# A quarter of the score masks goes from VectorE to ScalarE and GpSimd, with all order lists remade

## The chip, the cores and the metric

The kernel runs on one core of a Trainium2 chip. The metric is the device time of one execution in microseconds (us). Five engines matter: TensorE (PE, with its weight loads as PEld), VectorE (DVE), ScalarE (ACT), GpSimd (POOL) and SyncE (SP), which only issues DMAs here.

## The reference, cut to what matters

Sixteen sequences (batches) of 512 tokens by 256 features go through a block: layer norm, causal linear attention with 16 heads of 16, residual, layer norm, a mixture of experts with one shared and eight routed experts, residual.

```
q, k = elu(x Wq^T) + 1, elu(x Wk^T) + 1 ;  v = x Wv^T
out_i = q_i . sum_{j<=i} k_j v_j^T / (q_i . sum_{j<=i} k_j + 1e-8)
x = x + out Wo^T
x = x + sum_e cw[n,e] * (silu(x Wg_e) * (x Wu_e)) Wd_e + shared expert
```

## The kernel before

Each batch is cut into 4 chunks of 128 tokens. Within a chunk, attention is computed as a 128x128 matrix of scores per head, which is masked causally, and multiplied with v; across chunks it goes through running sums of k v^T ("state", used by "inter"). Products in reduced fp32 are made three times, of high and low halves (x3 in "scores", "k", "q", "gate", "up", "down").

The work is a list of named entries `name.i.b` for each engine (i: which part, b: which batch). Each engine runs its own list in order and waits on semaphores. `FIRST` is the start, `STEP` is repeated for t = 3 to 15 with the last number as a lag (batch t minus lag), and `LAST` is the end. The lists and the table `BANK`, which says which of six PSUM banks each product uses, are data; the code of the entries does not change.

The entries that the change and the prediction speak of:

- `piece.n` splits a loaded part of the weights: ScalarE copies the high half, GpSimd (for n=0 VectorE) subtracts it for the low half. Pieces 0 and 1 hold the weights of q and k, 2 and 3 those of v and of the output, 4 to 8 those of gate and up (pieces of 128x1024, the last 128x512), 9 to 11 those of down.
- `k.i`, `q.i`: TensorE's projection; ScalarE makes relu and exp (L661, L664); VectorE adds them (L861). `k_split.i`: ScalarE copies k_hi (L680), GpSimd subtracts for k_lo (L755). `q_split.i`: ScalarE q_hi (L674, two), VectorE q_lo (L867, two). `cum.i` is a scan on VectorE (L908).
- `scores.i` (i = 0 to 3, L1163) fills four banks at a time, and waits for k_lo, q_lo and for the four banks to be drained.
- `mask.j` (j = 0 to 15) drains the bank of one 128x512 tile of scores into the SBUF ring `scores` of 8 tiles. On VectorE it is one instruction that multiplies by the causal mask (L916). If `mask.j` stands in ScalarE's and GpSimd's lists, ScalarE copies the tile (L693), which frees the bank, and GpSimd then multiplies in SBUF (L767). `values.i` (L1180) waits for its four masked tiles.
- `gate`, `up`, `weigh` (L776), `split` (L725, L779) and `down` are the experts. A bank of `up.i` is drained by VectorE (L1018).
- `state`, `inter`, `wo`, `router`, `turn`, `warm`: the state products, their use, the output projection, the router, TensorE transposes, and idle transposes that only keep TensorE busy in the start.

In the kernel before, batches 0 and 1 send the odd masks (1, 3, ..., 15) through ScalarE and GpSimd; batches 2 to 15 have all 16 on VectorE.

Of the kernel before, what the change touches and what calls it, by code (L numbers as in the profile page):

```python
# [55 lines left out]
        q_split.0.0 up.1.2 q.1.0 result.0.3 mask.0.0 mask.3.0 den.0.0 mask.1.0 mask.2.0 at.1.1 den.1.0
        gate.4.2 at.0.1 gate.3.2 state.0.0 gate.5.2 up.4.2 up.5.2 wo.1.1 up.3.2 wo.0.1 ln2_stats.0.1
        mask.4.0 mask.7.0 ln2_apply.0.1 blocks.1.1 mask.5.0 mask.6.0 ln1_stats.0.-1 q_split.1.0 gate.8.2
        gate.7.2
# [8 lines left out]
        turn.1.0 turn.0.0 warm.8.0 k.0.0 q.0.0 k.1.0 v.0.0 v.1.0 q.1.0 scores.0.0 k_turn.0.0 warm.17.0  # L68
        scores.1.0 turn.1.1 k_turn.1.0 turn.0.1 values.0.0 state.0.0 scores.2.0 values.1.0 scores.3.0 k.0.1
        q.0.1 inter.0.0 inter.1.0 state.1.0 values.2.0 values.3.0 inter.2.0 inter.3.0 scores.0.1 q.1.1 k.1.1  # L70
        wo.1.0 wo.0.0 scores.1.1 k_turn.1.1 v.1.1 k_turn.0.1 v.0.1 state.0.1 values.0.1 scores.2.1 inter.1.1
        turn.2.0 turn.3.0 warm.10.0 inter.0.1 values.1.1 state.1.1 scores.3.1 gate.0.0 gate.1.0 turn.0.2
# [7 lines left out]
        turn.0.1 turn.1.1 wide.0.0 q_split.1.0 piece.9.0 mask.9.0 mask.11.0 mask.15.0 mask.13.0 wide.1.0  # L80
        k.0.1 q.0.1 piece.8.0 q_split.0.1 at.0.0 piece.10.0 mask.1.1 at.1.0 mask.3.1 q.1.1 k.1.1 wide.0.1
        mask.5.1 k_turn.1.1 v.1.1 mask.7.1 k_turn.0.1 v.0.1 q_split.1.1 mask.11.1 turn.2.0 mask.9.1 turn.3.0
        piece.11.0 ln1_apply.0.2 mask.15.1 gate.0.0 mask.13.1 gate.1.0 turn.0.2 turn.1.2 route.0.0 gate.2.0
        k.0.2 q.0.2 wide.1.1 q_split.0.2 split.0.0 k_split.0.2 k.1.2 v.1.2 k_turn.0.2 at.0.1 at.1.1 v.0.2
# [12 lines left out]
        q.1.0 mask.0.0 mask.2.0 cum.0.0 mask.6.0 mask.4.0 den.0.0 turn.0.1 turn.1.1 state.0.0 mask.10.0
        mask.8.0 den.1.0 mask.12.0 mask.14.0 spread.0.0 spread.1.0 k.0.1 mult.0.0 q.0.1 state.1.0 cum.0.1
        mult.1.0 mask.2.1 mask.0.1 den.0.1 q.1.1 k.1.1 wo.1.0 wo.0.0 mask.6.1 ln2_stats.0.0 mask.4.1
        ln1_stats.0.2 state.0.1 ln2_apply.0.0 cum.1.1 mask.10.1 mask.8.1 turn.2.0 turn.3.0 state.1.1  # L100
        mask.14.1 mask.12.1 den.1.1 spread.0.1 gate.0.0 turn.0.2 router.0.0 turn.1.2 gate.1.0 route.0.0
        rank0.0.0 rank1.0.0 gate.2.0 mult.0.1 up.0.0 q.0.2 spread.1.1 k.0.2 mult.1.1 q_split.0.2 up.1.0
        cum.0.2 k.1.2 cum.1.2 mask.0.2 mask.1.2 mask.3.2 up.2.0 q.1.2 den.0.2 mask.2.2 gate.4.0 gate.3.0
        den.1.2 up.4.0 gate.5.0 up.3.0 state.0.2 up.5.0 wo.0.1 wo.1.1 ln2_stats.0.1 mask.4.2 mask.5.2
        ln2_apply.0.1 blocks.1.1 mask.7.2 mask.6.2 ln1_stats.0.3 gate.8.0 q_split.1.2 gate.7.0
# [9 lines left out]
        up.5.13 wo.1.14 wo.0.14 down.0.13 scores.1.15 gate.6.13 down.2.13 gate.7.13 gate.8.13 down.1.13  # L115
        up.6.13 down.5.13 up.8.13 down.3.13 state.1.15 values.0.15 values.1.15 inter.1.15 scores.2.15
        up.7.13 down.4.13 gate.0.14 scores.3.15 down.6.13 router.0.14 gate.1.14 up.0.14 down.7.13 gate.2.14
        down.8.13 values.2.15 inter.0.15 inter.2.15 inter.3.15 values.3.15 gate.3.14 up.1.14 up.2.14 wo.0.15
        wo.1.15 gate.5.14 gate.7.14 gate.4.14 up.3.14 down.0.14 up.4.14 up.5.14 down.1.14 gate.8.14
        gate.6.14 down.2.14 up.8.14 down.3.14 up.6.14 up.7.14 down.4.14 router.0.15 gate.0.15 up.0.15  # L120
        gate.2.15 down.5.14 gate.1.15 down.7.14 up.2.15 down.6.14 gate.6.15 gate.3.15 up.1.15 gate.4.15
        up.3.15 up.4.15 down.8.14 gate.5.15 down.0.15 down.1.15 up.8.15 gate.7.15 up.6.15 up.5.15 down.2.15
        up.7.15 gate.8.15 down.4.15 down.3.15 down.5.15 down.7.15 down.6.15 down.8.15
# [1147 lines left out]
```

## Time and profile before

| | us |
|---|---|
| median of 3 runs (1010.31 to 1012.91) | 1011.97 |
| the profiled execution | 1008.9 |
| its span, first to last instruction | 1007.1 |
| PE busy | 986.0 (98%) |
| DVE busy | 876.0 (87%) |
| POOL busy | 595.9 (59%) |
| ACT busy | 446.8 (44%) |

Matmuls overlap in the records, so "busy" for PE is the union of their times. The profiled execution is 3.1 us below the median; 1.8 us of its time lie outside its span. A row of a group of instructions reads: line, engine, operation, output and inputs, shapes, count | busy us, mean ns | idle time of the engine ahead of them and what ended it.

### The profile page before, as it was taken

Reading aid. Unit: us, or ns where it says so; the run is one execution under the profiler, and the core shown is the slowest. Engines: PE = TensorE matmul, PEld = TensorE weight load, DVE = VectorE, ACT = ScalarE, POOL = GpSimd, SP = SyncE. Lnnn points to the kernel's source line nnn. Section 1 sums busy time; section 2 is a strip of 40 time slices with the busy share of each in tenths; the row PEclk is TensorE's granted clock in tenths of the full one; section 3 lists DMA queues with packets and bytes.
Section 4 is the critical chain, followed back from the end, with each engine's and each line's share of the span. In section 5 each row is a group of like instructions: output and inputs, shape, how many; then the busy total and the mean of one; then the engine's idle time right before and its main releaser. Section 6 shows DMA issues by size and latency. Waiting matters only on the chain.

```text
span 1007.1 us, 25374 instructions
## 1 busy us (share of the span) xinstructions
PE 986.0 (98%) x10037; PEld 847.2 (84%) x10037; DVE 876.0 (87%) x1832; ACT 446.8 (44%) x780; POOL 595.9 (59%) x470
## 2 busy tenths in 40 slices
...
GB/s 256 2 2 76 113 74 122 75 105 131 77 130 44 144 98 107 105 75 121 82 106 119 82 123 58 131 113 106 98 75 121 89 106 96 72 110 45 123 74 53
DMA packets 235604, 96.67 MB, mean 96 GB/s; under 512 B 161760, under 2 KB 217696, under 8 KB 235488
## 3 DMA queue, kind: packets, MB, share of 16 engines
...
## 4 chain that ended last, share of the span: by engine, by line
PE 92%; POOL 2%; DVE 2%; issue 1%; DMA 1%; ACT 0%; SPq 0%; DVEq 0%; POOLq 0%; ACTq 0%
PE bank L1044 56%; PE y_bank L1044 21%; PE bank L1180 6%; PE bank L1163 5%; PE bank L1196 2%; POOL wg_lo L737 1%; PE bank L1142 1%; DMA x_in<-in_x 1%; PE bank L1210 1%; POOL h_lo L779 0%; DVE scores L916 0%; DVE stats L796 0%; SPq L551 0%; POOL et L776 0%; DVE den L924 0%
## 5 line engine op out<-in xcount | busy, mean ns | idle before, releaser
L776 POOL TENSOR_TENSOR et<-et,cw_all 128x512 f32<-128x512 f32 x124 | 161.3, 1319 | 137.1 <-DVE et L1018 125.0
L1044 PE MATMUL bank<-xt_hi,wg_hi 128*128 128x512 f32 x576 | 235.0, 408 | 0.3 <-DVE scores L916 0.2
L1044 PE MATMUL bank<-xt_lo,wg_hi 128*128 128x512 f32 x576 | 227.9, 396 | 0.0
L1044 PE MATMUL bank<-xt_hi,wg_lo 128*128 128x512 f32 x576 | 227.9, 396 | 0.0
L779 POOL TENSOR_TENSOR h_lo<-et,h_hi 128x512 fp32r<-128x512 f32 x142 | 181.6, 1305 | 53.1 <-ACT h_hi L725 52.9
L916 DVE TENSOR_TENSOR scores<-bank,cst 128x512 f32<-128x512 f32 x240 | 152.4, 680 | 23.5 <-PE bank L1163 20.8
L1044 PE MATMUL y_bank<-wd_hi,h_hi 128*128 128x256 f32 x576 | 164.5, 286 | 0.0
L1044 PE MATMUL y_bank<-wd_lo,h_hi 128*128 128x256 f32 x576 | 161.3, 280 | 0.0
L1044 PE MATMUL y_bank<-wd_hi,h_lo 128*128 128x256 f32 x576 | 161.2, 280 | 0.0
L725 ACT ACTIVATE h_hi<-et 128x512 fp32r<-128x512 f32 x144 | 86.3, 627 | 147.8 <-POOL et L776 91.7
L716 ACT ACTIVATE et<-bank 128x512 f32<-128x512 f32 x144 | 84.2, 597 | 130.8 <-PE bank L1044 95.3
L1044 PEld LDWEIGHTS bank<-xt_hi,wg_hi 128*128 128x128 f32 x576 | 108.2, 188 | 30.3 <-issue 3.6
L1044 PEld LDWEIGHTS bank<-xt_hi,wg_lo 128*128 128x128 f32 x576 | 108.3, 188 | 26.2
L1044 PEld LDWEIGHTS bank<-xt_lo,wg_hi 128*128 128x128 f32 x576 | 108.7, 189 | 20.8
L1012 DVE SCALAR_TENSOR_TENSOR et<-et,bank 128x512 f32<-128x512 f32 x144 | 95.4, 679 | 29.1 <-ACT et L716 28.5
L1044 PEld LDWEIGHTS y_bank<-wd_hi,h_hi 128*128 128x128 f32 x576 | 108.3, 188 | 5.7
L764 POOL TENSOR_TENSOR cum<-cum,qf 128x512 f32<-128x512 f32 x32 | 41.7, 1304 | 119.7 <-DVE cum L908 119.7
L1044 PEld LDWEIGHTS y_bank<-wd_lo,h_hi 128*128 128x128 f32 x576 | 108.6, 189 | 1.9
L1044 PEld LDWEIGHTS y_bank<-wd_hi,h_lo 128*128 128x128 f32 x576 | 108.5, 188 | 0.0
L1018 DVE SCALAR_TENSOR_TENSOR et<-et,bank 128x512 f32<-128x512 f32 x144 | 94.9, 676 | 10.2 <-PE bank L1044 9.6
L674 ACT ACTIVATE q_hi<-qf,cst 128x512 fp32r<-128x512 f32 x56 | 37.3, 713 | 88.2 <-PE bank L1163 87.2
L1180 PE MATMUL bank<-scores,v_win 128*32 128x128 f32 x2048 | 65.8, 275 | 1.8 <-POOL scores L767 1.6
...
## 6 DMA issues: line engine op xcount, KB each, us to landing
cw_all<-cw_dram SPq DMA_DIRECT2D x124, 256.0 KB, 4.3
...
```

The costliest lines, as they stand in the source:

```text
L674: nc.scalar.activation(dst[:, j, :], qf[:, i, :], ACT.Copy, scale=cst[:, C_EO + j:C_EO + j + 1]).then_inc(q_half_done, 1)
L716: nc.scalar.activation(et[:, i % ET, :], bank[BANK["gate", i]][:, :], ACT.Tanh, scale=0.5)\
L725: nc.scalar.activation(h_hi[:, i % HR, :], et[:, i % ET, :], ACT.Copy).then_inc(h_hi_done, 1)
L764: nc.gpsimd.tensor_tensor(cum[:, i, :], cum[:, i, :], qf[:, i, :], ALU.mult).then_inc(qk_done, 1)
L776: nc.gpsimd.tensor_tensor(et[:, i % ET, :], et[:, i % ET, :], weights, ALU.mult).then_inc(weighed, 1)
L779: nc.gpsimd.tensor_tensor(h_lo[:, i % HR, :], et[:, i % ET, :], h_hi[:, i % HR, :].bitcast(f32), ALU.subtract).then_inc(h_lo_done, 1)
L916: nc.vector.tensor_tensor(scores[:, i % SM, :, :], bank[BANK["scores", i]][:, :].rearrange("p (h q) -> p h q", h=4), causal.unsqueeze(1).b ...
L1012: nc.vector.scalar_tensor_tensor(et[:, i % ET, :], et[:, i % ET, :], 1.0, bank[BANK["gate", i]][:, :], ALU.add, ALU.mult)\
L1018: nc.vector.scalar_tensor_tensor(et[:, i % ET, :], et[:, i % ET, :], 0.5, bank[BANK["up", i]][:, :], ALU.mult, ALU.mult)\
L1044: ins = nc.tensor.matmul(dst, l, r, start=first and n == 0, stop=last and n == 2, skip_group_check=shared)
L1163: last = nc.tensor.matmul(bank[BANK["scores", 4 * i + g]][:, j * 2 * P:(j + 1) * 2 * P] .rearrange("p (h q) -> p h q", h=2), keys[rows, m, ...
L1180: last = nc.tensor.matmul(bank[BANK["o", m]][32 * g:32 * g + 32, c * P:(c + 1) * P], v_win[:, c, 4 * m + g, h:h + 2, :].rearrange("p t d - ...
```

## The change

From batch 2 on, masks 1, 5, 9 and 13 are taken out of VectorE's list and put into ScalarE's and GpSimd's: 4 masks in 14 batches, 56 in all. Every other entry remains, with its engine and its count, on every engine. All lists are in a new order, `FIRST` now reaches further into the third step and `LAST` begins later, and `BANK` is new in part. The order written by hand at the very start (pieces 0, 1, 2, 3 first, on SP and ScalarE) is gone too. The core of the diff:

```
 "PE" STEP, before, from k.0.0:
-        down.6.3 k.0.0 q.0.0 up.2.2 k.1.0 up.1.2 q.1.0 v.0.0 down.7.3 down.8.3 scores.0.0 up.3.2 v.1.0
+        gate.2.2 down.6.3 k.0.0 q.0.0 k.1.0 up.2.2 q.1.0 up.1.2 gate.4.2 down.7.3 scores.0.0 down.8.3 v.0.0
+        gate.5.2 gate.3.2 v.1.0 up.4.2 up.5.2 up.3.2 state.0.0 wo.0.1 wo.1.1 down.0.2 scores.1.0 down.1.2
...
+        scores.2.0 up.7.2 down.5.2 down.4.2 scores.3.0 gate.0.1 router.0.1 values.2.0 inter.0.0 inter.1.0
+        values.3.0 inter.3.0 inter.2.0 gate.1.1 up.0.1
 "ACT" STEP
+        split.8.3 gate.1.2 gate.2.2 k.0.0 at.1.1 q.0.0 split.0.2 k.1.0 at.0.1 q_split.0.0 q.1.0 k_split.0.0
+        mask.1.0 split.2.2 split.1.2 gate.4.2 v.0.0 v.1.0 gate.5.2 gate.3.2 mask.5.0 split.5.2 q_split.1.0
+        split.3.2 split.4.2 wide.1.0 k_split.1.0 gate.6.2 gate.8.2 ln1_apply.0.-1 gate.7.2 take.2.1 mask.9.0
+        take.3.1 mask.13.0 wide.0.0 split.6.2 split.7.2 route.0.1 gate.0.1 take.1.-1 take.0.-1
 "POOL" STEP
+        qk.1.0 split.2.2 weigh.4.2 weigh.3.2 weigh.5.2 mask.1.0 rstd2.0.1 split.5.2 split.3.2 rstd1.0.-1
+        split.4.2 mask.5.0 k_split.1.0 weigh.8.2 weigh.6.2 take.2.1 take.3.1 mask.9.0 weigh.7.2 mask.13.0
+        split.7.2 split.6.2 take.1.-1 split.8.2 take.0.-1 split.0.1 qk.0.-1 k_split.0.-1 weigh.1.1 weigh.2.1
+        split.1.1
 "DVE" STEP, in part
+        mult.0.1 gate.1.2 up.0.2 mult.1.1 rank0.0.2 rank1.0.2 k.0.0 cum.0.0 q.0.0 gate.2.2 k.1.0 up.2.2
+        q_split.0.0 up.1.2 q.1.0 cum.1.0 mask.3.0 blocks.2.0 result.0.3 at.1.1 mask.2.0 den.0.0 mask.0.0
+        gate.4.2 at.0.1 den.1.0 up.4.2 gate.5.2 gate.3.2 state.0.0 up.3.2 up.5.2 wo.0.1 wo.1.1 ln2_stats.0.1
 FIRST, "ACT", "POOL" and "SP", their starts
-        piece.0.0 piece.1.0 piece.2.0 piece.3.0 turn.1.0 turn.0.0 piece.5.0 piece.4.0 k.0.0 q.0.0 k.1.0 piece.6.0 q_split.0.0
+        piece.2.0 piece.5.0 piece.0.0 piece.1.0 turn.1.0 piece.4.0 turn.0.0 piece.3.0 piece.6.0 piece.7.0
-        rstd1.0.0 piece.1.0 piece.2.0 piece.3.0 piece.4.0 rstd1.0.1 piece.5.0 piece.6.0 mask.1.0 piece.7.0 qk.0.0 mask.3.0
+        rstd1.0.0 piece.5.0 piece.1.0 piece.2.0 piece.4.0 piece.3.0 piece.7.0 rstd1.0.1 qk.0.0 piece.6.0
+        mask.3.0 mask.1.0 mask.7.0 mask.5.0 qk.1.0 mask.9.0 mask.11.0 piece.8.0 mask.15.0 mask.13.0 at.0.0
-        load_x.0.0 consts.0.0 piece.0.0 piece.1.0 piece.2.0 piece.3.0 consts.1.0 piece.5.0 piece.4.0 load_x.0.1 piece.7.0 piece.11.0
+        load_x.0.0 consts.0.0 piece.5.0 piece.2.0 piece.0.0 piece.1.0 piece.4.0 piece.3.0 piece.6.0
+        piece.7.0 load_x.0.1 small.0.0 consts.1.0 piece.9.0 piece.11.0 piece.8.0 load_x.0.2 piece.10.0
 BANK
-    ("o", 0): 3, ("o", 1): 2, ("q", 0): 5, ("q", 1): 5, ("router", 0): 1, ("scores", 0): 0, ("scores", 1):
+    ("o", 0): 3, ("o", 1): 2, ("q", 0): 5, ("q", 1): 4, ("router", 0): 1, ("scores", 0): 5, ("scores", 1):
+    2, ("scores", 2): 0, ("scores", 3): 1, ("scores", 4): 3, ("scores", 5): 1, ("scores", 6): 5, ("scores",
```

## Rows read from the trace of the kernel before

**Rows 1.** Windows: us; busy (count) of PE, PEld, DVE, ACT, POOL; PEclk, DMA share, GB/s
```profile
0.00:20.00 20.00, 13.45 (x79) 12.21 (x80) 10.58 (x32) 12.84 (x19) 12.84 (x17) 1.00 0.89 307
20.00:40.00 20.00, 14.97 (x195) 11.22 (x194) 16.52 (x22) 15.04 (x28) 19.73 (x12) 0.91 0.05 18
32.00:36.00 4.00, 3.39 (x44) 2.60 (x48) 3.93 (x3) 2.50 (x4) 4.00 (x4) 0.58 0.02 4
...
408.00:470.00 62.00, 61.60 (x647) 53.12 (x649) 56.34 (x120) 26.95 (x47) 36.30 (x30) 1.00 0.40 99
```

**Rows 2.** Waits of TensorE over the whole run: us, times, longest
```profile
PE bank L1163 <- issue: 3.8, 10, 0.5
```

**Rows 3.** The chain that ended last, four pieces: start, us, what
```profile
380.24 9.87 PE bank L1044 x48
393.87 8.65 PE bank L1044 x42
...
440.65 9.87 PE bank L1044 x48
454.74 8.65 PE bank L1044 x42
```

**Rows 4.** Groups of instructions over the whole run
```profile
L916 DVE TENSOR_TENSOR scores<-bank,cst 128x512 f32<-128x512 f32 x240 | 152.4, 680 | 23.5 <-PE bank L1163 20.8 <-POOL wg_lo L737 2.2
L867 DVE SCALAR_TENSOR_TENSOR q_lo<-qf,cst,q_hi 128x512 fp32r<-128x512 f32 x56 | 50.3, 938 | 0.0
L755 POOL TENSOR_TENSOR k_lo<-kf,k_hi 128x512 fp32r<-128x512 f32 x28 | 49.7, 1776 | 10.9 <-ACT k_hi L680 10.9
L767 POOL TENSOR_TENSOR scores<-scores,cst 128x512 f32<-128x512 f32 x16 | 20.3, 1287 | 2.7 <-ACT scores L693 2.7
L693 ACT ACTIVATE scores<-bank 128x512 f32<-128x512 f32 x16 | 9.3, 595 | 8.3 <-PE bank L1163 8.0 <-POOL wg_lo L737 0.2
```

**Rows 5.** The same chain in the window 409:471, between k.0 and scores.0
```profile
450.52 2.85 PE y_bank L1044 x24
453.37 0.39 issue
```

**Rows 6.** Timeline of one step, several engines: start, us, engine, instruction
```profile
440.49 0.40 PE L1044 MATMUL bank<-xa_hi,wa_hi 128*128 128x512 f32 x1
...
442.09 0.60 ACT L661 ACTIVATE expo<-bank 128x512 f32<-128x512 f32 x1 [2.21 <-PE bank L1044]
...
417.22 1.40 DVE L867 SCALAR_TENSOR_TENSOR q_lo<-qf,cst,q_hi 128x512 fp32r<-128x512 f32 x2
...
448.36 1.25 DVE L908 TENSOR_TENSOR_SCAN cum<-cst,kf 128x512 f32<-128x512 f32 x1
...
450.47 2.48 DVE L867 SCALAR_TENSOR_TENSOR q_lo<-qf,cst,q_hi 128x512 fp32r<-128x512 f32 x2
452.88 0.68 DVE L1018 SCALAR_TENSOR_TENSOR et<-et,bank 128x512 f32<-128x512 f32 x1
...
419.06 1.30 POOL L755 TENSOR_TENSOR k_lo<-kf,k_hi 128x512 fp32r<-128x512 f32 x1
...
448.50 2.21 POOL L755 TENSOR_TENSOR k_lo<-kf,k_hi 128x512 fp32r<-128x512 f32 x1
```

**Rows 7.** Timeline of the start: TensorE, then GpSimd
```profile
11.78 0.50 PE L1044 MATMUL bank<-xa_hi,wa_hi 128*128 128x512 f32 x1 [0.96 <-DVE xa_lo L840]
...
30.17 1.08 PE L1180 MATMUL bank<-scores,v_win 128*32 128x128 f32 x32 [1.43 <-POOL scores L767]
...
37.91 0.50 PE L1044 MATMUL bank<-xa_hi,wa_hi 128*128 128x512 f32 x1
...
8.46 4.47 POOL L737 TENSOR_TENSOR wa_lo<-cw_all,wa_hi 128x512 fp32r<-128x512 f32 x3 [1.16 <-ACT wa_hi L603]
13.50 2.41 POOL L737 TENSOR_TENSOR wg_lo<-scores,wg_hi 128x1024 fp32r<-128x1024 f32 x1 [0.56 <-ACT wg_hi L603]
...
28.66 3.72 POOL L767 TENSOR_TENSOR scores<-scores,cst 128x512 f32<-128x512 f32 x3
```

More of the change, by code:

```diff
@@ L40 @@
+        gate.5.2 gate.3.2 v.1.0 up.4.2 up.5.2 up.3.2 state.0.0 wo.0.1 wo.1.1 down.0.2 scores.1.0 down.1.2
+        down.2.2 gate.7.2 gate.6.2 gate.8.2 up.6.2 up.8.2 down.3.2 values.0.0 values.1.0 state.1.0
+        scores.2.0 up.7.2 down.5.2 down.4.2 scores.3.0 gate.0.1 router.0.1 values.2.0 inter.0.0 inter.1.0
+        values.3.0 inter.3.0 inter.2.0 gate.1.1 up.0.1
         """,
     "ACT": """
-        gate.7.3 gate.6.3 gate.8.3 ln1_apply.0.0 wide.0.1 take.3.2 take.2.2 split.7.3 split.8.3 split.6.3
@@ L56 @@
[L56 to L59, printed above, removed]
+        mask.10.1 mask.8.1 mask.14.1 mask.15.1 mask.12.1 router.0.2 spread.0.1 route.0.2 gate.0.2 spread.1.1
+        mult.0.1 gate.1.2 up.0.2 mult.1.1 rank0.0.2 rank1.0.2 k.0.0 cum.0.0 q.0.0 gate.2.2 k.1.0 up.2.2
@@ L60 @@
+        q_split.0.0 up.1.2 q.1.0 cum.1.0 mask.3.0 blocks.2.0 result.0.3 at.1.1 mask.2.0 den.0.0 mask.0.0
+        gate.4.2 at.0.1 den.1.0 up.4.2 gate.5.2 gate.3.2 state.0.0 up.3.2 up.5.2 wo.0.1 wo.1.1 ln2_stats.0.1
+        mask.4.0 mask.6.0 ln2_apply.0.1 blocks.1.1 ln1_stats.0.-1 mask.7.0 q_split.1.0 gate.8.2 gate.6.2
+        up.8.2 up.6.2 gate.7.2 blocks.0.-1 state.1.0 up.7.2 mask.11.0
         """,
     "SP": """
-        load_x.0.-1 cw_load.7.3 cw_load.6.3 put.1.2 cw_load.5.3 get.1.2 put.0.0 get.0.0 cw_store.0.2
@@ L63 @@
-        cw_load.1.2 cw_load.0.2 cw_load.2.2 put.2.0 get.2.0 store.0.3 cw_load.4.2 cw_load.3.2
+        cw_store.0.2 cw_load.0.2 cw_load.1.2 put.2.0 cw_load.2.2 cw_load.3.2 store.0.3 cw_load.4.2 get.2.0
+        cw_load.5.2 put.1.1 cw_load.7.2 get.1.1 cw_load.6.2 put.0.-1 get.0.-1 load_x.0.-2
         """,
@@ L67 @@
     "PE": """
[L68 to L72, printed above, removed]
@@ L73 @@
-        turn.1.2 router.0.0 gate.2.0 k.0.2 values.2.1 values.3.1 inter.3.1 inter.2.1 q.0.2 up.0.0 v.1.2
-        up.1.0 k.1.2 q.1.2 k_turn.0.2 v.0.2 scores.0.2 up.2.0 state.0.2 gate.3.0 gate.4.0 up.4.0 gate.5.0
-        up.3.0 k_turn.1.2
+        warm.8.0 turn.1.0 turn.0.0 warm.17.0 q.0.0 k.0.0 k.1.0 v.0.0 v.1.0 q.1.0 scores.0.0 scores.1.0
+        k_turn.0.0 turn.0.1 warm.10.0 turn.1.1 k_turn.1.0 state.0.0 values.0.0 scores.2.0 values.1.0
+        inter.1.0 inter.0.0 scores.3.0 k.0.1 q.0.1 state.1.0 values.2.0 inter.2.0 values.3.0 inter.3.0 q.1.1
@@ new lines @@
+        scores.0.1 k.1.1 wo.0.0 wo.1.0 scores.1.1 v.1.1 v.0.1 k_turn.0.1 k_turn.1.1 values.0.1 state.0.1
+        turn.2.0 scores.2.1 turn.3.0 inter.0.1 state.1.1 inter.1.1 values.1.1 scores.3.1 gate.0.0 router.0.0
+        gate.1.0 turn.0.2 turn.1.2 values.2.1 inter.2.1 inter.3.1 values.3.1 up.0.0 k.0.2 gate.2.0 q.0.2
+        k.1.2 q.1.2 v.1.2 v.0.2 up.1.0 up.2.0 gate.4.0 k_turn.0.2 scores.0.2 down.0.0 gate.3.0 state.0.2
+        gate.5.0 up.4.0 up.3.0 up.5.0 wo.1.1 wo.0.1 gate.7.0 scores.1.2 down.1.0 gate.6.0 down.2.0 gate.8.0
@@ L76 @@
+        k_turn.1.2 up.8.0 up.6.0 up.7.0 values.0.2 values.1.2 inter.1.2 state.1.2 scores.2.2 down.5.0
+        down.4.0 down.3.0 scores.3.2 gate.0.1 inter.0.2 router.0.1 values.2.2 inter.2.2 inter.3.2 values.3.2
+        gate.1.1 up.0.1
         """,
     "ACT": """
-        piece.0.0 piece.1.0 piece.2.0 piece.3.0 turn.1.0 turn.0.0 piece.5.0 piece.4.0 k.0.0 q.0.0 k.1.0 piece.6.0 q_split.0.0
-        v.1.0 q.1.0 mask.1.0 piece.7.0 v.0.0 mask.3.0 ln1_apply.0.1 k_turn.0.0 mask.5.0 mask.7.0 k_turn.1.0
@@ L80 @@
[L80 to L84, printed above, removed]
@@ L85 @@
-        k_split.1.2 q.1.2 split.1.0 split.2.0 gate.3.0 gate.4.0 gate.5.0 k_turn.1.2 split.4.0 split.5.0
-        split.3.0 wide.1.2 q_split.1.2
+        piece.2.0 piece.5.0 piece.0.0 piece.1.0 turn.1.0 piece.4.0 turn.0.0 piece.3.0 piece.6.0 piece.7.0
+        q.0.0 k.0.0 k.1.0 q_split.0.0 v.0.0 v.1.0 q.1.0 mask.3.0 mask.1.0 ln1_apply.0.1 mask.7.0 mask.5.0
+        turn.0.1 wide.0.0 k_turn.0.0 q_split.1.0 turn.1.1 k_turn.1.0 piece.8.0 mask.11.0 mask.9.0 piece.11.0
+        piece.9.0 mask.13.0 wide.1.0 mask.15.0 k.0.1 q.0.1 at.0.0 q_split.0.1 piece.10.0 at.1.0 mask.3.1
@@ new lines @@
+        k.1.1 mask.1.1 q.1.1 wide.0.1 mask.7.1 mask.5.1 q_split.1.1 v.1.1 v.0.1 k_turn.1.1 k_turn.0.1
+        ln1_apply.0.2 turn.2.0 mask.11.1 turn.3.0 mask.9.1 mask.15.1 mask.13.1 wide.1.1 route.0.0 gate.0.0
+        gate.1.0 turn.1.2 turn.0.2 k.0.2 gate.2.0 q.0.2 k_split.0.2 k.1.2 q_split.0.2 v.1.2 v.0.2
+        k_split.1.2 split.0.0 q.1.2 k_turn.0.2 at.1.1 split.1.0 at.0.1 gate.4.0 gate.3.0 mask.1.2 split.2.0
+        gate.5.0 q_split.1.2 split.4.0 mask.5.2 split.3.0 split.5.0 wide.1.2 gate.6.0 k_turn.1.2 gate.8.0
@@ L87 @@
+        gate.7.0 ln1_apply.0.3 mask.9.2 take.2.1 take.3.1 split.7.0 wide.0.2 mask.13.2 route.0.1 split.6.0
+        gate.0.1 take.1.3 take.0.3
         """,
     "POOL": """
-        rstd1.0.0 piece.1.0 piece.2.0 piece.3.0 piece.4.0 rstd1.0.1 piece.5.0 piece.6.0 mask.1.0 piece.7.0 qk.0.0 mask.3.0
-        mask.7.0 mask.5.0 qk.1.0 piece.9.0 mask.11.0 mask.9.0 mask.15.0 mask.13.0 at.0.0 qk.0.1 at.1.0
-        mask.3.1 mask.1.1 piece.10.0 mask.5.1 rstd2.0.0 mask.7.1 qk.1.1 rstd1.0.2 piece.11.0 mask.15.1
@@ L92 @@
-        mask.9.1 mask.13.1 mask.11.1 k_split.0.2 split.0.0 piece.8.0 weigh.1.0 qk.0.2 split.1.0 weigh.2.0
-        qk.1.2 at.1.1 split.2.0 at.0.1 weigh.4.0 weigh.5.0 weigh.3.0 rstd2.0.1
+        rstd1.0.0 piece.5.0 piece.1.0 piece.2.0 piece.4.0 piece.3.0 piece.7.0 rstd1.0.1 qk.0.0 piece.6.0
+        mask.3.0 mask.1.0 mask.7.0 mask.5.0 qk.1.0 mask.9.0 mask.11.0 piece.8.0 mask.15.0 mask.13.0 at.0.0
+        qk.0.1 at.1.0 piece.9.0 mask.3.1 rstd1.0.2 mask.1.1 mask.7.1 rstd2.0.0 qk.1.1 piece.11.0 mask.5.1
@@ L94 @@
+        piece.10.0 mask.11.1 mask.9.1 mask.13.1 mask.15.1 k_split.0.2 qk.0.2 split.0.0 weigh.1.0 qk.1.2
+        split.1.0 weigh.2.0 at.0.1 at.1.1 split.2.0 mask.1.2 weigh.4.0 weigh.3.0 weigh.5.0 rstd2.0.1
+        split.3.0 split.4.0 split.5.0 rstd1.0.3 mask.5.2 k_split.1.2 weigh.8.0 weigh.6.0 weigh.7.0 take.2.1
+        take.3.1 mask.9.2 mask.13.2 split.7.0 split.6.0 take.1.3 take.0.3 split.8.0 split.0.1 qk.0.3
+        k_split.0.3 weigh.2.1 weigh.1.1 split.1.1
         """,
     "DVE": """
-        ln1_stats.0.0 ln1_apply.0.0 piece.0.0 turn.1.0 turn.0.0 ln1_stats.0.1 k.0.0 q.0.0 k.1.0 cum.1.0
@@ L97 @@
[L97 to L105, printed above, removed]
+        ln1_stats.0.0 ln1_apply.0.0 piece.0.0 turn.1.0 turn.0.0 ln1_stats.0.1 q.0.0 k.0.0 cum.0.0 k.1.0
@@ new lines @@
+        cum.1.0 q.1.0 mask.0.0 mask.2.0 den.0.0 mask.6.0 mask.4.0 turn.0.1 spread.0.0 state.0.0 turn.1.1
+        mask.8.0 mask.10.0 den.1.0 mask.14.0 spread.1.0 mult.0.0 mask.12.0 k.0.1 state.1.0 q.0.1 cum.0.1
+        mult.1.0 ln1_stats.0.2 mask.2.1 den.0.1 k.1.1 wo.0.0 mask.0.1 wo.1.0 q.1.1 ln2_stats.0.0 mask.4.1
+        mask.6.1 ln2_apply.0.0 cum.1.1 state.0.1 turn.2.0 mask.10.1 mask.8.1 turn.3.0 state.1.1 den.1.1
+        mask.14.1 router.0.0 mask.12.1 spread.0.1 route.0.0 turn.1.2 gate.0.0 gate.1.0 turn.0.2 mult.0.1
@@ L106 @@
+        rank0.0.0 k.0.2 rank1.0.0 gate.2.0 spread.1.1 q.0.2 mult.1.1 cum.0.2 up.0.0 k.1.2 q_split.0.2
+        cum.1.2 up.1.0 q.1.2 up.2.0 den.0.2 mask.3.2 mask.2.2 den.1.2 gate.4.0 mask.0.2 ln1_stats.0.3
+        gate.3.0 state.0.2 up.3.0 gate.5.0 up.4.0 up.5.0 wo.1.1 wo.0.1 ln2_stats.0.1 mask.4.2 mask.6.2
+        ln2_apply.0.1 blocks.1.1 mask.7.2 q_split.1.2 gate.8.0 gate.6.0 gate.7.0 up.6.0 up.7.0 up.8.0
+        blocks.0.3 state.1.2 mask.11.2
         """,
     "SP": """
-        load_x.0.0 consts.0.0 piece.0.0 piece.1.0 piece.2.0 piece.3.0 consts.1.0 piece.5.0 piece.4.0 load_x.0.1 piece.7.0 piece.11.0
@@ L114 @@
     "PE": """
[L115 to L123, printed above, removed]
+        down.6.13 down.7.13 gate.2.14 down.8.13 up.2.14 up.1.14 gate.3.14 wo.1.15 wo.0.15 down.0.14
@@ L124 @@
+        gate.4.14 gate.7.14 down.1.14 gate.5.14 up.4.14 up.5.14 up.3.14 gate.6.14 down.2.14 up.7.14 up.6.14
+        gate.8.14 down.4.14 up.8.14 down.5.14 router.0.15 gate.0.15 up.2.15 gate.1.15 down.7.14 gate.2.15
+        down.3.14 gate.4.15 up.0.15 down.6.14 down.8.14 gate.6.15 up.1.15 gate.3.15 up.4.15 up.3.15
+        gate.5.15 down.0.15 gate.7.15 up.6.15 down.1.15 up.5.15 up.8.15 down.2.15 up.7.15 gate.8.15
+        down.4.15 down.3.15 down.5.15 down.7.15 down.6.15 down.8.15
         """,
@@ L131 @@
-        split.5.15 gate.8.15 split.7.15 split.6.15 split.8.15
+        split.8.13 gate.1.14 split.0.14 at.1.15 gate.2.14 at.0.15 gate.3.14 split.1.14 gate.4.14 split.2.14
+        gate.5.14 split.4.14 split.3.14 gate.6.14 split.5.14 gate.7.14 take.3.15 gate.8.14 take.2.15
+        split.7.14 route.0.15 split.6.14 split.8.14 gate.0.15 gate.1.15 gate.2.15 split.0.15 gate.3.15
+        split.1.15 gate.4.15 split.2.15 split.3.15 gate.5.15 split.4.15 gate.7.15 gate.6.15 split.5.15
+        gate.8.15 split.7.15 split.6.15 split.8.15
@@ L132 @@
         """,
     "POOL": """
[L134 to L138 removed]
+        rstd2.0.15 weigh.4.14 split.2.14 weigh.3.14 split.4.14 split.3.14 weigh.5.14 split.5.14 take.3.15
@@ L139 @@
+        take.2.15 weigh.7.14 weigh.8.14 split.7.14 weigh.6.14 split.6.14 split.8.14 weigh.2.15 weigh.0.15
+        split.0.15 weigh.1.15 split.1.15 weigh.3.15 split.2.15 weigh.4.15 split.3.15 split.4.15 weigh.5.15
+        split.5.15 split.6.15
         """,
     "DVE": """
-        gate.6.13 up.8.13 up.6.13 state.1.15 mask.9.15 mask.8.15 up.7.13 mask.10.15 mask.11.15 mask.12.15
-        mask.13.15 mask.15.15 mask.14.15 router.0.14 spread.0.15 route.0.14 rank0.0.14 rank1.0.14
-        result.0.13 gate.0.14 mult.0.15 spread.1.15 up.0.14 at.0.15 mult.1.15 gate.2.14 gate.1.14 at.1.15
```

59 lines of the change are left out of this document (18 added, 41 removed).

## The prediction

> **What bounds the kernel now.** I read the busy times first, then the chain that ended last, then TensorE's own waits, and only then the engines that feed it. In a window of one step and a bit, TensorE is busy 61.60 of 62 us, VectorE 56.34, GpSimd 36.30 and ScalarE 26.95 [rows 1]. So taking work from VectorE, the second busiest engine, gives nothing by itself: time comes back only where TensorE stands still. The reader is to see how little that is. Over the run TensorE is idle 1007.1 - 986.0 = 21.1 us. Of these 6.55 us lie in the first 20 us and 5.03 us in the next 20 [rows 1]. In the steady part one kind of wait is left: ahead of L1163, the scores, 10 times, 3.8 us in all [rows 2]. The chain puts it down to "issue", but the timeline shows what was late. It lies between 453.37 and 453.76 us [rows 5], ahead of scores.0. VectorE's q_lo ran from 450.47 for 2.48 us, and behind it up.1, whose bank 1 scores.0 needs (scores 2 stands in bank 1), from 452.88 to 453.56 [rows 6]. So VectorE is late there. How much: from the start of k.0's run to that of the long run after scores.0 takes 454.74 - 440.65 = 14.09 us in this step and 393.87 - 380.24 = 13.63 us in a step without the wait [rows 3]. 0.46 us are lost, and of the 13 steps between 100 and 900 us I count 8 like the first: 3.7 us.
>
> **The masks.** 56 masks leave VectorE: 56 x 0.68 = 38.1 us of busy time, 2.7 per batch. ScalarE gets 56 x 0.595 = 33.3 us and GpSimd 56 x 1.287 = 72.1 us, 5.2 per batch [rows 4]. Per 62 us that makes VectorE about 53.6, GpSimd about 41.5 and ScalarE about 29.5, all below TensorE. Direct effect on the end: 0, as TensorE's matmuls cover all of it. No DMA is added or taken away. If the cover were gone, a masked tile would come 0.595 + 1.287 = 1.88 us after its scores, plus what stands in GpSimd's list ahead of it, where VectorE took 0.68. The tightest place is mask.13.0 for values.3.0: weigh.7.2 is ahead of it on GpSimd, and between them TensorE has gate.0, router, values.2 and two inters, about 1.4 + 0.4 + 0.9 + 0.7 = 3.4 us. The path needs at most 0.6 + 1.3 + 1.3 = 3.2 us. It holds by 0.2 us at the worst, by more if weigh.7 is done early.
>
> **The steady step, from k.0 to scores.0.** This decides the 3.7 us. Prices for TensorE: from k.0 to v.0 the chain has 48 matmuls in 9.87 us, six groups of 6 and v.0 (12 short ones), and 24 short ones (two downs) in 2.85 us, so 1.43 for a down or v and (9.87 - 1.43)/6 = 1.41 for a k, q, gate or up [rows 3, 5]. Before, k.0 starts at 440.49 [rows 6] and scores.0 could start at 453.37: 12.88 us. After, k.0, q.0, k.1, up.2, q.1, up.1, gate.4 are seven groups and down.7 one: 7 x 1.41 + 1.43 = 11.3 us. So TensorE comes 1.6 us earlier, counted from k.0, while VectorE was 0.46 us late already: it must be 2.0 us quicker. It is: cum.1 (1.25) and the copies of k (about 1.0), which stood ahead of q_lo, stand behind it now. That gives 2.2 us; and where GpSimd holds its hands off, q_lo takes 1.40 us instead of 2.48 [rows 6], 1.1 us more. Against them stands gate.2 (0.6), now inside the stretch. up.1 was done at 453.56 - 440.49 = 13.1 us, and will be at 13.1 - 2.2 - 1.1 + 0.6 = 10.4 us, 0.9 us early.
>
> The other input is k_lo, on GpSimd. I follow ScalarE's new list from its first relu, 442.09 - 440.49 = 1.60 us after k.0 starts [rows 6]: k.0 (2 x 0.63), at.1, q.0 (2 x 0.63), split.0, k.1 (2 x 0.63), at.0, q_split.0 (1.32), q.1 (2 x 0.63). With 0.55 for each copy (its 0.595 [rows 4] less the overlap with the next), k_split.0 starts at 1.60 + 4 x 1.26 + 3 x 0.55 + 1.32 less overlaps of 0.1 at three places, 9.3 us, and ends at 9.9. GpSimd's k_lo then takes 1.30 us if it is alone (419.06) and 2.21 if VectorE is at a scan of SBUF (448.50, beside 448.36) [rows 6]. So k_lo is there at 11.2 to 12.1 us, against 11.3 us: a wait of 0 to 0.9 us in each step. I take 0.2, nearer to the lower end, since the new scan (cum.1) starts after up.1 and q.1, at about 10.8 us, when k_lo is already under way.
>
> Next on the same step: state and wo.0. GpSimd has weigh.1, weigh.2, split.1, qk.1 in one run, and VectorE between them q.1, cum.1, mask.3, copies, result, at.1, mask.2, den.0, mask.0, gate.4, at.0, den.1, up.4, gate.5. Adding their steps (0.6 each; cum 1.2, copies 1.0, result 1.2, den 1.9) from 10.4 us gives 23.0 us for gate.5, whose bank 1 wo.0 needs. TensorE reaches wo.0 at 11.3 + 1.0 + 11.3 (eight groups) + 0.4 = 24.0 us. 1.0 us is left, and at.1, at.0 and the scan can each lose some 0.3 to 0.6 to GpSimd: a wait of 0 to 0.5; I take 0.1. TensorE's total per step is 0.3 us of waits, 13 x 0.3 = 3.9 us, against 3.7 before: +0.2 us, bounds -3.7 (no wait left) and 13 x (0.9 + 0.5) - 3.7 = +14.5.
>
> **The port.** The trace shows that the same instruction takes 1.40 or 2.48 us (q_lo) and 1.30 or 2.21 us (k_lo) [rows 6]; on average 938 and 1776 ns [rows 4]. The slow ones stand where the other of the two engines works from SBUF. The added GpSimd products read and write SBUF alone, whereas the mask that they replace reads PSUM. So the change adds 5.2 us per batch in which such a collision can happen. The Trainium skill, SBUF — State Buffer, section "SBUF: two separate sides", says that VectorE and GpSimd share a port pair under an exclusive lock, held for a whole instruction, taken by GpSimd's instructions and by VectorE's with two SBUF inputs. The rows agree: k_lo's extra 0.91 us is less than the whole scan that began ahead of it, 1.25. By that rule a k_lo that begins first is not slowed, which is the lower of my two ends for it; the rule speaks against the change as a whole, as each added product can block an all-SBUF instruction of VectorE for up to 1.3 us.
>
> **The start.** First matmul of q, k: before at 11.78 us [rows 7]. After, piece.5 (512 KB) and piece.2 (256 KB) are loaded ahead of pieces 0 and 1: 768 KB at 307 GB/s [rows 1], 2.5 us. On GpSimd piece.5 stands ahead of piece.1: 2.41 us [rows 7]. ScalarE copies 2 and 5 ahead of 0 and 1 (0.6 + 1.0); I put the end of its copy of 5 at 10.2 us, by the loads. These lie partly beside each other; I get the first matmul at 14.6 us, +2.9. Next, v.0 waits for piece.3, which is behind pieces 5, 1, 2 and 4 on GpSimd: from 10.2 us, 2.4 + 1.5 + 1.5 + 2.4 + 1.5 = 19.5 to 20.3 us (1.5 is 4.47/3 [rows 7]), so q.1 ends at 24.5 instead of 20.4 us: +4.1. But then TensorE waited anyway: values.0 started at 30.17, 1.43 us late, for GpSimd's masks [rows 7]. After, GpSimd has the same pieces and masks to do: it starts them 1.7 us later (10.2 against 8.46) but loses less in between; its masks 1 and 3 end at 29.5 to 31 us, and values.0 starts at 30.5 to 32. The odd masks are done at 32.1 to 33.6 against 32.38. The start of k.0 of batch 1 comes at about 38.1 to 39.0 us, with both inters of batch 0 (0.7 us) already done, against 37.91 before [rows 7]. So of 4 us all but -0.5 to +0.5 are absorbed. Later lists of the start: the last idle transposes (10, about 1.1 us) now stand where TensorE waits anyway: up to -1. The window 32 to 36 shows a granted clock of 0.58, so part of it at the lower of the two levels (1.2 GHz), [rows 1]; ahead of it TensorE had stood still for 1.43 us and more [rows 7]. The same can fall elsewhere or away: -1.7 to +3. I take +0.8 for the start, bounds -3 and +5.
>
> **The end.** `LAST` keeps its last entries (down.8.15 and the stores) and their waits: 0, bounds -1 and +1.
>
> **Sum**, on the profiled execution: 1008.9 + 0 (masks) + 0.2 (steps) + 0.8 (start) + 0 (end) = 1009.9. The median of the runs stands 3.1 us above the profiled one, so 1013.0 us.
>
> **Rivals.** (a) The sum above, no change that can be told (0.3% is 3 us, about what the measurement tells apart): chance 0.42. (b) k_lo or a bank comes late in every step. The GpSimd list is so full that k_lo collides (+0.9 us), or gate.5 is late (+0.5); with 0.8 us of waits per step, 13 x 0.8 - 3.7 = +6.7, with the start 1019.5. For it: TensorE comes to scores.0 1.6 us sooner, and k_lo has a margin of 0.1 us. Against: the rest of the step has margins near 1 us. It decides from 0.5 us per step. Chance 0.28. By the page's lock each added mask that blocks a VectorE instruction costs at most 1.3 us of VectorE, 5.2 per step against about 62 - 53.6 = 8 us of room: the bound would still not pass to VectorE. (c) The start is not absorbed: +4.1 us stay, 1012 + 4 = 1016. For it: the first v and q are that late. Against: GpSimd's pieces end the later wait. Chance 0.10. (d) The other side: VectorE's relief takes away the wait at scores.0 wholly, -3.7, and the idle transposes -1: 1012 - 4.7 = 1007.3. For it: VectorE is late there in 8 of 13 steps, and has 2.7 us less to do per batch. It decides if k_lo comes within 11.3 us. Chance 0.20.
>
> **Numbers.** Faster 0.20 is (d). Slower is (b), (c) and little else, 0.38. Same 0.42. The range reaches from (d), 1007, to a little past (b), 1020; the likeliest case alone is 1010 to 1015.
>
> **What would show it.** L916 x184, L693 and L767 x72. PE's "L1163 <- issue" and any wait on k_lo or on L1018: 3.7 us if right, near 0 by (d), 8 or more by (b). q_lo's mean nearer to 700 ns, k_lo's mean above or below 1776. First projection at 14.6 us, but k.0 of batch 1 near 38.5. The period of the step: 60.6 us. It would be wrong if DMAs got in (get.2.0 now stands behind two loads and a store on SP's queue, with about 1 us of room ahead of state.0), or if TensorE's clock fell in the start.

## The result and the profile after

The changed kernel takes 1046.14 us (median of 4 runs, 1043.86 to 1048.70); the kernel before took 1011.14 us in the same comparison. The ratio is 1.0348, 95% interval 1.0327 to 1.0368: 35 us slower. The forecast was 1013.0 us with a range of 1007 to 1020. The profiled execution has a span of 1045.7 us against 1007.1.

The groups first, which answer to [rows 4] (line, engine, operation, shapes, count | busy us, mean ns | idle before, releaser):

```profile
L919 DVE TENSOR_TENSOR scores<-bank,cst 128x512 f32<-128x512 f32 x184 | 119.3, 682 | 20.2 <-PE bank L1166 19.7
L870 DVE SCALAR_TENSOR_TENSOR q_lo<-qf,cst,q_hi 128x512 fp32r<-128x512 f32 x56 | 42.5, 799 | 6.2 <-ACT q_hi L677 6.2
L758 POOL TENSOR_TENSOR k_lo<-kf,k_hi 128x512 fp32r<-128x512 f32 x28 | 36.1, 1289 | 37.3 <-ACT k_hi L683 37.3
L770 POOL TENSOR_TENSOR scores<-scores,cst 128x512 f32<-128x512 f32 x72 | 92.9, 1295 | 8.3 <-ACT scores L696 8.2
L696 ACT ACTIVATE scores<-bank 128x512 f32<-128x512 f32 x72 | 42.5, 597 | 251.5 <-PE bank L1166 251.2
```

The masks are where they were meant to go, at the forecast price each. q_lo and k_lo are both faster than before: each of the 28 k_lo takes 1.27 to 1.30 us, the length that it had undisturbed in [rows 6]. Nothing here explains 35 us. TensorE's waits do (engine, line, what it waited for: us in total, times, longest):

```profile
PE bank L1145 <- issue: 28.8, 13, 3.2
...
PE bank L1166 <- issue: 1.0, 3, 0.4
```

L1145 is the state product, a place where the kernel before had no such wait; of the one ahead of the scores (now L1166), 3.8 us in [rows 2], 1.0 us is left. As before, "issue" only says that nothing in the profile was seen to release TensorE. The queue of SP shows what was late, in one step (start, us, SP's DMA issues):

```profile
469.08 2.56 SPq L581 DMA_DIRECT2D k_dram<-blocks  x4
471.74 1.06 SPq L574 DMA_DIRECT2D cw_all<-cw_dram  x2
472.84 0.94 SPq L597 DMA_DIRECT2D out_y<-x_mid  x2
473.89 0.49 SPq L574 DMA_DIRECT2D cw_all<-cw_dram  x1
474.49 0.82 SPq L588 DMA_DIRECT2D k_tok<-k_dram  x1
```

The same place in the kernel before:

```profile
450.57 2.30 SPq L578 DMA_DIRECT2D k_dram<-blocks  x4
454.85 0.38 SPq L585 DMA_DIRECT2D k_tok<-k_dram  x1
```

And the chain of the changed kernel at that place, with TensorE's last work ahead of the state product (start, us, what):

```profile
468.91 9.90 PE bank L1047 x54
478.81 1.97 issue
480.77 0.40 PE bank L1145 x21
```

The put (put.2.0) writes blocks of k to DRAM in four parts, and the load of k_tok (get.2.0) reads them back for the state product. Ahead of the load SP now issues three loads of routing weights (cw_all, 256 KB each) and the store of a result (out_y, two transfers of 256 KB). The load is issued 474.49 - 469.08 = 5.41 us after the first part of the put, 4.28 before. Then it takes longer, by the table of DMA issues on both pages of the profile (KB each, median us to landing), the kernel after first:

```profile
k_tok<-k_dram SPq DMA_DIRECT2D x13, 384.0 KB, 6.2
```

```profile
k_tok<-k_dram SPq DMA_DIRECT2D x13, 384.0 KB, 3.8
```

5.41 + 6.2 = 11.6 us, so it lands at 480.7, and the state product starts at 480.77. TensorE was ready 478.81 - 469.08 = 9.7 us after the put began. The wait is 2 us in this step; over the 13 steps it is 1.6 to 3.2 us, 28.8/13 = 2.2 on average.

The second loss follows the wait. In two steps, the wait and the same 24 matmuls behind it (chain over the run):

```profile
289.88 2.49 issue
292.77 4.47 PE bank L1047 x24
...
354.17 2.21 issue
356.78 3.06 PE bank L1047 x24
```

and the windows at the first of them (us; busy of PE, PEld, DVE, ACT, POOL; granted clock, DMA share, GB/s):

```profile
288.00:292.00 4.00, 1.88 (x9) 1.17 (x7) 1.87 (x3) 0.00 (x0) 1.29 (x1) 1.00 0.92 299
292.00:294.00 2.00, 1.63 (x34) 1.62 (x35) 1.10 (x4) 0.00 (x0) 0.00 (x0) 0.98 0.03 9
294.00:296.00 2.00, 2.00 (x12) 2.00 (x11) 1.84 (x4) 0.00 (x0) 1.22 (x1) 0.50 0.00 0
296.00:298.00 2.00, 2.00 (x14) 2.00 (x14) 0.69 (x1) 0.00 (x0) 2.00 (x3) 0.67 0.00 0
```

TensorE stands still, goes on, and from 294 to about 297 us runs at a granted clock of 0.50, the lower level (1.2 GHz): 4.47 instead of 3.06 us for the same matmuls. Not every wait is followed by it, and its length alone does not tell: behind the one of 2.21 us nothing was lost, behind one of 1.97 us (at 478.81) the 24 matmuls took 4.56 us. By the same chain the 24 matmuls take 4.45 to 5.31 us in 8 of the 13 steps and 3.06 or 3.07 in the other five: 12.5 us more over the run.

All together, from one down product to the same one twelve steps later (chain, kernel after):

```profile
171.14 3.02 PE y_bank L1047 x24
...
934.52 3.06 PE y_bank L1047 x24
```

and eleven steps later in the kernel before:

```profile
167.10 3.01 PE y_bank L1044 x24
...
834.39 3.01 PE y_bank L1044 x24
```

A step takes (934.52 - 171.14)/12 = 63.6 us, against (834.39 - 167.10)/11 = 60.7. The difference, unrounded 2.95 us, times 12 is 35 us: the loss lies in the steps, not in the start or the end.

### The profile page after: what moved, and what is told of

Read it like the earlier page. It is cut to its first block, busy times and chain, and to the rows that moved or that the text cites. A ratio compares the mean times of both kernels' runs of the same rounds, so it can differ in the third digit from the quotient of the medians.

```text
span 1045.7 us, 25574 instructions
## 1 busy us (share of the span) xinstructions
PE 997.6 (95%) x10037; PEld 863.4 (83%) x10037; DVE 885.7 (85%) x1776; ACT 459.0 (44%) x836; POOL 661.9 (63%) x526
## 4 chain that ended last, share of the span: by engine, by line
PE 89%; issue 4%; DVE 4%; DMA 1%; ACT 1%; SPq 1%; DVEq 0%; ACTq 0%
PE bank L1047 54%; PE y_bank L1047 20%; PE bank L1166 5%; PE bank L1183 5%; PE bank L1199 2%; DMA x_in<-in_x 1%; PE bank L1213 1%; PE bank L1145 1%; DVE stats L799 1%; DVE scores L919 0%; SPq L554 0%; DVE cum L911 0%; PE bank L1100 0%; DVE kf L864 0%; DVE minus_mean L831 0%
## 5 line engine op out<-in xcount | busy, mean ns | idle before, releaser
L782 POOL TENSOR_TENSOR h_lo<-et,h_hi 128x512 fp32r<-128x512 f32 x142 | 190.7, 1349 | 160.9 <-ACT h_hi L728 160.9
L779 POOL TENSOR_TENSOR et<-et,cw_all 128x512 f32<-128x512 f32 x124 | 170.0, 1386 | 117.0 <-DVE et L1021 111.5
L696 ACT ACTIVATE scores<-bank 128x512 f32<-128x512 f32 x72 | 42.5, 597 | 251.5 <-PE bank L1166 251.2
L919 DVE TENSOR_TENSOR scores<-bank,cst 128x512 f32<-128x512 f32 x184 | 119.3, 682 | 20.2 <-PE bank L1166 19.7
L770 POOL TENSOR_TENSOR scores<-scores,cst 128x512 f32<-128x512 f32 x72 | 92.9, 1295 | 8.3 <-ACT scores L696 8.2
```

The lines of the kernel that those rows point to most:

```text
L696: nc.scalar.activation(scores[:, i % SM, :, :].rearrange("p h q -> p (h q)"), bank[BANK["scores", i]][:, :], ACT.Copy)\
L770: nc.gpsimd.tensor_tensor(scores[:, i % SM, :, :], scores[:, i % SM, :, :], causal.unsqueeze(1).broadcast_to([P, 4, P]), ALU.mult).then_in ...
L779: nc.gpsimd.tensor_tensor(et[:, i % ET, :], et[:, i % ET, :], weights, ALU.mult).then_inc(weighed, 1)
L782: nc.gpsimd.tensor_tensor(h_lo[:, i % HR, :], et[:, i % ET, :], h_hi[:, i % HR, :].bitcast(f32), ALU.subtract).then_inc(h_lo_done, 1)
L919: nc.vector.tensor_tensor(scores[:, i % SM, :, :], bank[BANK["scores", i]][:, :].rearrange("p (h q) -> p h q", h=4), causal.unsqueeze(1).b ...
```

## The experiments

All medians are compared with the kernel before in the same comparison (1011.1 to 1011.5 us).

**1. The load of k_tok directly behind its put.** Only one entry of SP's `STEP` list moves.

```
-        put.2.0 cw_load.2.2 cw_load.3.2 store.0.3 cw_load.4.2 get.2.0 cw_load.5.2
+        put.2.0 get.2.0 cw_load.2.2 cw_load.3.2 store.0.3 cw_load.4.2 cw_load.5.2
```

> Theory A: the loss is the load of k_tok (get.2.0), which SP's new list puts behind two loads of routing weights, the store of a result and a third load. It lands 6.2 us after its issue instead of 3.8, and state.0 waits some 2.2 us in each of 13 steps (28.8 us), after which the granted clock falls in part of them (some 12 us more). With get.2.0 right behind put.2.0 it is issued about 1 us earlier and has nothing ahead of it: 1003 to 1012 us, wait ahead of the state product under 3 us, granted clock back to 0.99 or more. Rival B (the masks' longer way, GpSimd and the shared port) or C (the new order of TensorE as such): still over 1035 us. Rival D: SP now blocks on the put and the routing weights come late instead: 1015 to 1030 us.

Measured: 1005.36 us, ratio 0.9943 (0.9922 to 0.9964). The load is issued 4.8 us after the put's start and lands after 3.3 us; TensorE has no wait at the state product at all and, in the profiled execution, a granted clock of 0.998. SP's queue in one step:

```profile
451.44 2.91 SPq L581 DMA_DIRECT2D k_dram<-blocks  x4
456.26 0.38 SPq L588 DMA_DIRECT2D k_tok<-k_dram  x1
456.74 0.96 SPq L574 DMA_DIRECT2D cw_all<-cw_dram  x2
```

One entry gives back 1046.14 - 1005.36 = 40.8 us, more than the whole loss, so all else in the change together is a gain of 6 us. Theory A holds. Rival D (routing weights late) does not show.

**2. What lies ahead of it: the store or the loads.** First the store alone is moved behind the get, then everything but the store.

```
 first:
-        cw_load.2.2 cw_load.3.2 store.0.3 cw_load.4.2 get.2.0 cw_load.5.2
+        cw_load.2.2 cw_load.3.2 cw_load.4.2 get.2.0 store.0.3 cw_load.5.2
 second:
-        put.2.0 cw_load.2.2 cw_load.3.2 store.0.3 cw_load.4.2 get.2.0
+        put.2.0 store.0.3 get.2.0 cw_load.2.2 cw_load.3.2 cw_load.4.2
```

> The new lists with only store.0.3 (two transfers of 256 KB) moved behind get.2.0; the three loads of routing weights stay ahead. If it is bytes and issue time ahead of the load of k_tok that make it late, taking away two of five transfers gives about 1 us at the issue and 1 to 1.5 us at the landing: state wait 0 to 8 us over the run instead of 28.8, landing 4 to 5.2 us, 1006 to 1018 us. If only the loads of routing weights matter (many short packets): still above 1030 us.

> The new lists with store.0.3 alone between put.2.0 and get.2.0; all three loads of routing weights behind the get. In e4_store_late the get was issued as early as in e1_get_first (4.9 against 4.8 us after the start of the put) and still landed after 6.2 instead of 3.3 us, with three loads of 256 KB ahead. If it is their packets ahead of the load of k_tok that hold it up, the store, issued early and nearly done, costs little: landing 3.3 to 4.3 us, state wait under 3 us, 1004 to 1009 us. If any 512 KB ahead does: landing 5 us or more, 1012 us or more.

Measured: with only the loads ahead 1019.63 us (ratio 1.0084, 1.0059 to 1.0109), landing 6.2 us, state wait 15.0 us in 13 times, at most 2.1 us, granted clock 0.999 in the profiled execution. With only the store ahead 1004.67 us (0.9946, 0.9929 to 0.9963), landing 3.5 us, no state wait. The first is a miss of my range, and the telling one. Its SP queue:

```profile
457.94 2.91 SPq L581 DMA_DIRECT2D k_dram<-blocks  x4
462.81 0.37 SPq L588 DMA_DIRECT2D k_tok<-k_dram  x1
```

The get is issued 4.87 us after the put's start, as early as in experiment 1, and lands 2.9 us later than there. So the three loads of 256 KB ahead in the DMA engines were worth 2.9 us of the lateness, and the longer issue on SP 0.5 us in this step (5.41 against 4.87) and 0.8 on average over the 13 (5.49 against 4.65).

The store alone costs the load 0.2 us at the landing and some 0.5 us at the issue (5.2 us after the put's start on average, against 4.6 in experiment 1), and both fit into the 1.8 us of room that experiment 1 leaves (9.7 - 4.6 - 3.3). The two runs do not separate the kind of the transfers from their bytes and their times: the loads are 768 KB, issued from 1.9 us ahead on, the store is 512 KB, issued from 2.4 us ahead on.

The Trainium skill, DMA: Bandwidth & Descriptors, section "Queues, rings and completion order", says that on each of the 16 engines descriptors are consumed in ring order. The run with the loads ahead agrees (6.2 against 3.3 us); the one with the store ahead does not contradict it, since the store, issued from 454.34 us on, lands after 3.1 us (median of its two transfers), within some 1.3 us of the load's issue at 456.74.

With the loads ahead the waits are 1.15 us on average, and in the profiled execution none is followed by slower matmuls, not even the two longest (2.06 and 2.08 us). Its other executions show granted clocks of 0.996 to 0.998 and are 3 to 6 us longer than the profiled one, so that some clock may have been lost in them.

**3. A like order of SP in the kernel before.** The load stands behind two loads of routing weights and the store (three and the store in the new lists).

```
-        put.2.0 get.2.0 store.0.3 cw_load.4.2 cw_load.3.2
+        put.2.0 cw_load.2.2 store.0.3 cw_load.4.2 get.2.0 cw_load.3.2
```

(cw_load.2.2 stood ahead of put.2.0 before.)

> The kernel before with get.2.0 behind a load of routing weights, the store and another load, as in the new list. In it state.0 comes 12.8 us after the start of the put, 3.1 us later than in the new order. If the slack in TensorE's order decides together with SP's order: 1008 to 1016 us and the state wait under 5 us. If SP's order alone decides: 1030 us or more.

Measured: 1011.82 us, ratio 1.0008 (0.9998 to 1.0017). The load lands after 6.0 us here too, and no state wait appears. In the kernel before, 463.39 - 450.57 = 12.8 us lie between the put's start and the state product; in the changed one TensorE is ready for it after only 9.7. So it takes both parts of the remade lists: SP's order, by which the load lands 11.6 instead of 4.28 + 3.8 = 8.1 us after the put's start in the changed kernel, and TensorE's, which asks for it 3.1 us sooner.

**4. Filling the wait.** 18 idle transposes into the state's bank ahead of each state.0 from batch 3 on.

```
                 elif name == "state":
+                    if i == 0 and b >= BEGIN:
+                        for _ in range(18):
+                            nc.tensor.transpose(bk[:, 0:P], ident, ident)
```

> The new lists, with 18 idle transposes of TensorE into the state's bank ahead of each state.0 from batch 3 on, about 2 us that fall into the wait. If the wait costs twice (once as a wait, once as a lower clock after it), the granted clock is back at 0.99 or more and the time falls by the second part alone: 1028 to 1037 us. If the clock does not follow from the wait: 1044 to 1050 us, clock 0.983 to 0.985.

Measured: 1031.37 us, ratio 1.0201 (1.0178 to 1.0223), granted clock 1.000 instead of 0.983. The load lands as late as before (6.4 us), so the waiting remains, but doing useless work in it gives back 1046.14 - 1031.37 = 14.8 us. That is the price of the lower clock; counted on the 24 matmuls behind each wait it is 12.5. The waits (28.8) and these come to 41 to 44 us; experiment 1 gave 40.8.

**5. Are the masks a gain, a loss or nothing?** With the masks back on VectorE (mask.1, 5, 9, 13 next to their neighbours), once in the lists of the change and once with the load also moved:

```
 DVE STEP
-        mask.3.0 ... mask.4.0 ... mask.11.0 ... mask.14.1
+        mask.1.0 mask.3.0 ... mask.5.0 mask.4.0 ... mask.11.0 mask.9.0 ... mask.13.1 mask.14.1
 ACT, POOL STEP
-        mask.1.0, mask.5.0, mask.9.0, mask.13.0
```

> The new lists with the 56 masks back on VectorE. Theory A: SP's list is as late as before, so at least as slow: 1040 to 1055 us, state wait still 25 us or more. Rival B (masks through ScalarE and GpSimd cost the time): 1010 to 1020 us.

> As e1_get_first, and the 56 masks back on VectorE, in the new order. If the masks' move is what lets the new order run without waits (VectorE has 2.7 us less per batch): 1012 to 1030 us, with TensorE waiting on VectorE (k, q or up). If the masks' move costs nothing and brings nothing: 1003 to 1008 us.

Measured: 1074.53 us (ratio 1.0614, 1.0576 to 1.0652) and 1022.77 us (1.0111, 1.0081 to 1.0141). The first is slower even than I expected, with 35.0 us of state waits; so the masks' way through ScalarE and GpSimd is not what cost the time. The second is 17.4 us slower than experiment 1, from which it differs by the masks alone. Waits of its TensorE:

```profile
PE bank L1049 <- DVE scores L921: 5.1, 7, 1.0
PE bank L1215 <- DVE scores L921: 4.8, 12, 0.4
```

In the new order VectorE's masks drain the banks too late for the next products, which shows as 9.9 us of waits in the profiled execution (the fastest of the four, 1017.83 us); moved masks are worth 17 us there by the medians.

In the lists of the kernel before, the masks alone, first with those of batch 2 and then without its mask.1 and mask.5:

```
 DVE STEP: mask.1.0, mask.5.0, mask.9.1, mask.13.1 taken out
 ACT STEP
+        k_split.1.0 mask.1.0 ... mask.5.0 q_split.1.0 ... take.2.2 mask.9.1 ... split.6.3 mask.13.1
 POOL STEP
+        split.2.2 mask.1.0 ... rstd2.0.1 mask.5.0 ... weigh.6.3 mask.9.1 mask.13.1
```

> The lists of the kernel before with only the 56 masks moved to ScalarE and GpSimd. Theory A: the masks cost nothing: 1006 to 1014 us, the wait ahead of scores.0 smaller than 3.8 us. Rival B: 1020 us or more.

> As e3_masks_only (1020.3 us), but mask.1 and mask.5 of batch 2, which stand in the first lists, stay on VectorE. If e3's loss is a matter of where I put those two (its steps took 60.9 us on average from 173 us on, and the first 173 us were 6.4 us longer): 1010 to 1015 us. If the moved masks cost in every step: still 1018 us or more.

Measured: 1020.25 us (1.0081, 1.0063 to 1.0099) and 1015.58 us (1.0052, 1.0031 to 1.0073). Both miss what I expected of theory A. The first lies in the range of rival B, that the moved masks cost time in the old order; the second misses its range by 0.6 us. 3 to 5 us were a matter of where I put two entries in the first lists (4.7 by the medians, 2.9 by the ratios). The rest is in the steps of the second kernel, by its chain:

```profile
166.93 3.02 PE y_bank L1047 x24
...
837.92 3.01 PE y_bank L1047 x24
```

(837.92 - 166.93)/11 = 61.0 us against 60.7, some 4 us in 13 steps. The wait ahead of the scores did not go (4.2 us, 10 times), and one ahead of the values came (1.1 us). So the moved masks bring nothing and cost a little in an order that was made without them.

**6. The start.** Experiment 1 with pieces 0 to 3 first on SP, ScalarE and GpSimd, as before.

```
-        load_x.0.0 consts.0.0 piece.5.0 piece.2.0 piece.0.0 piece.1.0 piece.4.0 piece.3.0 ...
+        load_x.0.0 consts.0.0 piece.0.0 piece.1.0 piece.2.0 piece.3.0 consts.1.0 piece.5.0 ...
```

> As e1_get_first (1005.4 us), and the first lists in the order of the kernel before: pieces 0 to 3 first on SP, ScalarE and GpSimd. If the late first projection (15.2 us against 11.8) is absorbed by GpSimd's masks as forecast: 1004 to 1006.5 us. If it is paid in full: 1001 to 1003 us.

Measured: 1005.48 us (0.9945, 0.9930 to 0.9961), against 1005.36: the same, although the first projection begins at 12.83 us instead of 15.15.

## Why the prediction was wrong

The masks (0 direct): right. 56 x 0.597 and 56 x 1.295 us, as priced, and hidden in the new order. In the old one they cost 4 us (experiment 5).

k_lo and scores.0 (0 to 0.9 us of wait, 0.2 taken): the mechanism was right at its lower end. k_lo's mean is 1289 ns, undisturbed in every batch, q_lo's 799 instead of 938, and the wait ahead of the scores, 3.8 us in [rows 2], is 1.0. What the prediction expected of the port shows in one step of the kernel after: k_lo begins at 464.68 and takes 1.30 us, and the scan that begins behind it, at 465.50, takes 1.56 instead of the 1.23 of a scan beside an idle GpSimd (458.61). One reading of the rows was loose: the 1.40 and 2.48 us of q_lo in [rows 6] are for two instructions, the mean of 938 ns is for one. The sum does not depend on it. wo.0 (0.1 taken) shows no wait of note either.

The start (+0.8, bounds -3 and +5): right. The first projection began at 15.17 us (14.6 forecast) and k.0 of batch 1 at 38.84 (38.1 to 39.0 forecast), and experiment 6 shows that the lateness is absorbed. The lower clock in the start stayed as it was, 0.91 over 20 to 40 us in both kernels.

The step that failed is a term that is not in the sum. The prediction names get.2.0 only under what would make it wrong, "behind two loads and a store on SP's queue, with about 1 us of room ahead of state.0", and costs it at nothing. There are three loads and a store ahead of it, and how it came to 1 us is not shown. What hides the load is the stretch of TensorE's work between the put and the state product, 9.7 us. With the issue after 5.4 us and the landing of the kernel before, 3.8 us, in which nothing stood ahead of the load, 0.5 us of room would have been left. But the landing took 6.2 us. SP's queue, the only one that the prediction names, was worth 0.5 to 0.8 us, the transfers ahead in the DMA engines 2.9 (experiment 2). So the room of 1 us became 2.2 us of wait on average, 13 times: 28.8 us.

The second failure is that a wait of TensorE was priced by its length alone. 28.8 us of standing still cost another 12 to 15 us of lower clock (experiments 1 and 4).

The rivals: (b) had the right sign but the wrong place and size, and (c), a start that is not absorbed, did not happen. (d), the opposite side, was what the rest of the change does: with the late load mended 1005.4 us, against 1007.3 forecast for it, and no wait ahead of the scores from 100 us on. That wait was 3.8 us of the gain of 6; where the remainder comes from was not traced. "Taking work from VectorE [...] gives nothing by itself" holds for the old order, where it cost 4 us, but it says nothing of what the relief makes possible: with VectorE's old load the new order would lose 17 us.

Open: with the store alone ahead (experiment 2) four steps in the middle of the run are 0.1 to 1.0 us longer than the others of 60.2 us, in experiment 1 three are 1.0 us longer, and why is not known. That the lower clock follows some waits and not other ones of the same length is seen, not explained.
